# Which heads of an attention layer are turned by TensorE and which by DMA

## The reference, cut to what matters

```python
q = (x @ Wq + bq).reshape(1, B * N, H, hd)              # 1024 queries, 16 heads of 16
kv = (cond @ Wkv + bkv).reshape(1, -1, 2, H, hd)        # 1024 keys and values
q = _fq_sym(q * scale, axis=-1); k = _fq_sym(k, axis=-1); v = _fq_sym(v, axis=2)
attn = jax.nn.softmax(jnp.einsum('bhqd,bhkd->bhqk', q, k), axis=-1)
attn = _fq_unsigned(attn, axis=-1)                      # rounded to 255 levels of the row's maximum
out = jnp.einsum('bhqk,bhkd->bhqd', attn, v)
out = out.transpose(0, 2, 1, 3).reshape(B, N, C) @ Wp + bp
```

## Time and profile before

| | before |
|---|---|
| median of 3 runs | 450.31 us (449.9 to 451.88) |
| profiled execution, its own time | 452.0 us |
| its span | 450.2 us |
| PE / DVE / ACT / POOL busy | 307.4 / 365.1 / 324.3 / 124.9 us |
| mean granted TensorE clock | 0.86 of full |
| steps 0 to 127 (first to last exponential's start) | 190.98 to 378.80 us |

### The profile page before, as it was taken

One profiled execution on the slowest core, in us unless ns is written; L12 is line 12 of the kernel. 1 busy time (PEld: TensorE's weight loads), 2 busy tenths in 40 slices (PEclk: granted clock), 3 DMA queues, 4 the chain that ended last, 5 costly groups with the idle time before them and its releaser, 6 DMA issues.

```text
span 450.2 us, 7440 instructions
## 1 busy us (share of the span) xinstructions
PE 307.4 (68%) x2594; PEld 192.4 (43%) x2594; DVE 365.1 (81%) x597; ACT 324.3 (72%) x513; POOL 124.9 (28%) x260
## 2 busy tenths in 40 slices
PE   4999986774365877657577676877776777526445
PEld 2666554421264766433344443444443445203334
DVE  4758998299999683758699899899999997678975
ACT  3387689772234544799799999899999999467751
POOL 3703544000200111101212231223222312278760
PEclk9989999596596996978889999799899989755856
DMA  8600022000020001126999998889899959000001
GB/s 284 284 1 1 2 93 95 0 1 0 1 93 0 2 0 25 23 48 134 246 135 178 168 155 130 147 151 158 138 163 142 179 112 157 1 1 1 23 23 48
DMA packets 115637, 39.91 MB, mean 89 GB/s; under 512 B 110480, under 2 KB 114192, under 8 KB 114832
## 3 DMA queue, kind: packets, MB, share of 16 engines
q1 hardware_dynamic: 115168, 38.85, 43.9%
q0 software_dynamic: 144, 0.52, 0.3%
q10 hardware_dynamic: 288, 0.07, 0.1%
HBM read 11.11 MB, written 1.05 MB: 27 GB/s over the span
## 4 chain that ended last, share of the span: by engine, by line
DVE 28%; ACT 23%; PE 18%; issue 17%; POOL 9%; DMA 3%; POOLq 1%; SPq 0%; DVEq 0%; ACTq 0%
ACT rb L796 15%; DVE nm L1229 4%; POOL ra L524 4%; PE ps L1745 3%; DVE xn L895 2%; PE ps L1721 2%; POOL small L529 2%; ACT ra L850 2%; PE ps L1757 2%; DMA tern<-rb 2%; DVE rb L1154 2%; DVE rb L1141 2%; DVE gs L1132 2%; DVE rb L1152 2%; DVE st L886 1%
## 5 line engine op out<-in xcount | busy, mean ns | idle before, releaser
L1229 DVE TENSOR_REDUCE nm<-ps 128x1 f32<-128x1024 f32 x128 | 153.4, 1218 | 19.8 <-PE ps L1745 19.0
L796 ACT ACTIVATE rb<-ps,eb,sq 128x1024 int16<-128x1024 f32 x128 | 153.8, 1215 | 9.1 <-POOL eb L502 8.4
L1745 PE MATMUL ps<-ra,rb 128*128 128x512 bf16 x256 | 84.7, 418 | 41.0 <-ACT rb L796 40.4
L502 POOL TENSOR_SCALAR eb<-nm,sq 128x1 f32<-128x1 f32 x128 | 34.5, 270 | 148.5 <-DVE nm L1229 147.8
L1745 PEld LDWEIGHTS ps<-ra,rb 128*128 128x128 bf16 x256 | 16.2, 101 | 59.6 <-ACT rb L796 57.1
L1770 PEld LDWEIGHTS ps<-ra,tern 128*128 128x128 f16 x624 | 25.9, 98 | 17.5 <-issue 4.0
L1770 PE MATMUL ps<-ra,tern 128*128 128x16 f16 x624 | 26.3, 171 | 2.1 <-DMA tern<-rb 2.0
L796 ACT ACTIVATION_READ_ACCUMULATOR rb<-ps,eb,sq 128x1 f32 x128 | 27.0, 211 | 0.0
L1624 PE MATMUL ps<-xqT,tern 128*128 128x512 bf16 x64 | 19.8, 453 | 9.8 <-DVE rb L1141 8.5
L1644 PE MATMUL ps<-idb,gs 128*128 128x128 bf16 x64 | 7.7, 295 | 26.5 <-DVE gs L1324 26.5
L1757 PEld LDWEIGHTS ps<-idh,rb 128*128 128x128 f16 x256 | 17.9, 105 | 16.9 <-issue 10.6
(11 more groups left out here) (202 smaller groups left out, 727.1 us busy)
## 6 DMA issues: line engine op xcount, KB each, us to landing
stage<-w SPq DMA_DIRECT2D x2, 1024.0 KB, 4.7
rb<-ra SPq DMA_DIRECT2D x16, 128.0 KB, 2.9
rb<-wide_rows SPq DMA_DIRECT2D x1, 1536.0 KB, 7.1
xs<-x SPq DMA_DIRECT2D x4, 256.0 KB, 4.5
cx<-ctx_in SPq DMA_DIRECT2D x4, 256.0 KB, 4.7
stage<-w_gate SPq DMA_DIRECT2D x1, 1024.0 KB, 7.4
stage<-w_up SPq DMA_DIRECT2D x1, 1024.0 KB, 10.2
stage<-w_down SPq DMA_DIRECT2D x1, 1024.0 KB, 4.6
```

What stands on the lines that cost most here:

```text
L502: nc.gpsimd.tensor_scalar(eb[:, u % 3:u % 3 + 1], nm[:, u % 3:u % 3 + 1], sq[:, t, h:h + 1], LN255, ALU.mult, ALU.add).then_inc(s_bias, 1)
L796: A(esc[u % E_RING], bank(2 * (u % 3), 2), ACT.Exp, bias=eb[:, u % 3:u % 3 + 1], scale=sq[:, t, h:h + 1], accum_out=es[:, t % 2, h:h + 1]) ...
L1229: V.tensor_reduce(nm[:, u % 3:u % 3 + 1], bank(2 * (u % 3), 2), AX.X, ALU.max, negate=True).then_inc(s_max, 1)
L1745: ins = M(bank(2 * (u % 3) + hf), qz[t % 2][:, h // 2, h % 2, :], kT[:, h // 2, 512 * hf:512 * hf + 512], start=True, stop=True)
```

## The change

One constant changes, and with it who turns which head in each tile:

```diff
-ON_TENSOR = (1, 4, 12, 15)
+ON_TENSOR = (1, 6, 12)
```

## The result

The changed kernel takes 467.86 us (median of 4 runs, 462.82 to 470.24), beside 451.1 us for the kernel before on the same chip (449.9 to 452.16): 1.033 times as long, 95% interval 1.028 to 1.039. Run once more later it took 467.01 beside 452.15, 1.032 (1.027 to 1.036). The forecast was 461.0 us. 467.86 lies 0.9 us above the range of 455 to 467; the ratio on the forecast's own base, 1.033 x 450.31, is 465.3. The profile shown here is of the longest execution of the changed kernel, 470.24 us (span 468.4, clock 0.80); a second one, of 466.61 us (clock 0.82), was taken with the later run, and where the two differ both are given.

The account below looks back on a forecast made before the run. It took VectorE's maxima and ScalarE's exponentials to bound the attention loop. Tile 0 -0.45, tile 1 +0.75, even tiles +3.45, odd +5.85 and clock +1.1 made +10.7 on 450.31: 461.0 us, range 455 to 467 (own 457 to 464.5).

Parts of the forecast that it names:

- The new wait: Step 9, tiles 1 to 7: `o_transposes` waits for head 6's move on ScalarE, 1.95 us a boundary (bounds 0.47, 2.6).
- S: Start of head 8's exponential on ScalarE, from which the times at a tile's boundary are counted.
- Which wait ends last: Same boundary: head 10's exponential, behind TensorE's late scores, at S + 4.6; head 9's, about S + 2.65, is not last.
- The saved moves: Moves of heads 15 and 4 leave ScalarE: 0.8 us less per even tile, 0 in tiles 3, 5, 7.
- Tile 0: No boundary there; the move behind head 6 goes, saving 0.45 us that everything behind inherits.
- The clock: The new wait's idle stretch in each tile lowers TensorE's clock: 1.1 us in sum, bounds 0 and 10.5.
- rival C: The stall drops the clock for the heads behind it in most of seven tiles: +17.1, 467.4 us; chance 0.12.
- DMA: SP's queue keeps up, if narrowly, with 13 transposes a tile: 0, at worst 1.8 us per even tile.
- Rival B: DMA becomes the bound at 13 transposes: 1.8 us per even tile, +4.6, 454.9 us; chance 0.08.
- The end: Tile 7's head 15, now turned by DMA, lands near 383.8, before VectorE's scaling at 384.32: 0, at most 0.7 us.
- The sum: All tiles and the clock together: +10.7 us on the median 450.31, so 461.0 us.

Follow-up runs that it names:

- the filling: Changed kernel with 12 more matmuls of 256 columns, into an unread part of bank 6, ahead of each `o_transposes`: 464.94 us; again 462.95 us, 1.022 of before.

## Why the prediction was right, and where its sizes were off

*The new wait.* Right in place, releaser and count: seven waits before L1778 for L783, and none with heads 1, 4 and 12. With head 5 there are six, which cost little since they end one exponential and one move sooner. Its arithmetic for one boundary was S + 1.87 for `o_transposes` and S + 4.6 for head 10. Measured at full clock (tile 6): 4.43, so 1.79 us instead of 1.95. At the lower clock, in the six others, `o_transposes` came at S + 1.93 as well, but its two transposes, the scores (1.06 us for 0.60) and their maxima brought head 10 to S + 5.10: 2.46 us, near the bound of 2.6. I had priced all seven at full clock. This is the largest miss, 6 x 0.66 = 4.0 us (4 x 0.66 = 2.6 in the second profile). The idling itself I put at 1.5 us each, and it was 1.2; the price never hung on it.

*Which wait ends last.* Predicted, TensorE's, with head 9 "not last". Shown by `o_out` one step later: head 9 came 1.24 us sooner, head 10 not at all.

*The saved moves.* 0.8 us taken for an even tile; 0.55, 0.20 and 0.39 measured, in the second profile 0.40, 0.21 and 0.55. With head 15 alone gone heads 0 to 8 take 10.48 us (10.90 before) where the clock holds, and with head 4's move gone too at best 10.36. So the first move is worth 0.42 and the second 0.12. That behind it the turn through three pairs of banks sets the pace, as the prediction feared, fits this, but no run isolates it. In the odd tiles heads 0 to 8 stayed at 12.79 to the hundredth, as VectorE's fullness there said. Tile 1 saved 1.5 where 1.2 was forecast.

*Tile 0.* Forecast -0.45; measured +0.34, and -0.44 in the second profile. Head 6's move also stands behind head 8 there, which I had not counted: heads 8 to 10 took 2.86 us where it was 2.44. Heads 10 to 15 took 0.42 less and made up for it, so that the forecast came out by luck. In the first profile TensorE was slow at its step 9 besides, and heads 8 to 10 took 3.53.

*The clock.* I put 1.1 us on it, behind head 9, and named a fall in most tiles as rival C (467.4). What came lies between, and the larger part of C's clock came with it. The clock falls ahead of the wait: in six of seven tiles, in both profiles, the scores of step 9 already took about 1.04 us. Tile 1 is the exception, at 0.61; in the first profile the clock fell during its wait. Tile 2 of after, `o_transposes` still to come:

```profile
257.74 0.61 PE L1745 MATMUL ps<-ra,rb 128*128 128x512 bf16 x2 [0.88 <-ACT rb L796]
258.93 0.81 PE L1745 MATMUL ps<-ra,rb 128*128 128x512 bf16 x2 [0.58 <-ACT rb L796]
260.11 1.04 PE L1745 MATMUL ps<-ra,rb 128*128 128x512 bf16 x2 [0.38 <-ACT rb L796]
...
263.39 0.66 PE L1778 MATMUL ps<-idf,rb 128*128 128x128 f32 x2 [0.97 <-ACT stage L783]
```

What differs behind the wait is whether the clock is back. The scores of step 10 took 1.06 us in six boundaries of the first profile and four of the second, the ones that took 5.09 or 5.10 us, and 0.59 in the others. With the filling in the wait's place they took 0.59 to 0.62 in all seven, in both profiles, though five of the seven had come to it with scores of 1.03 us or more. So it is TensorE's idling there that keeps the clock down.

From head 10 on all tiles together lost only 0.1 us, 0.3 in the second profile, but that is luck of the comparison: tiles 1, 2 and 5 lost 2.2 us, and the profile of before had a fall of its own in tile 3, which gave 2.1 back. With the filling the same stretches took 52.9 us where the changed kernel's took 55.5 and 55.7. So the lower clock cost the changed kernel some 6 us in the first profile, 4.0 in the boundaries and 2.2 behind them, where I had put 1.1.

Steps 7 and 8 now hold nothing but scores: the `attend`s of the new tile are not due yet, and head 4's transposes, which stood at step 7, are gone. That the fall comes from this is likely and not shown: in the kernel with the filling these steps are the same, and in tiles 4 and 6 the clock held at them in both profiles. With head 5 the clock fell in the same place (tile 2) and 8 to 10 took 2.98 there, where the other tiles mostly had 2.75: little, without the wait behind it.

*DMA.* Costed at nothing for 13, right: tiles 2 and 4 in 20.9 us with 13, and at 14 a ratio of 1.003 whose interval holds 1. Rival B's sign, `attend` waiting for landed transposes, was there three times in the loop (4.9 us), as before (three, 4.4). The Trainium skill's page "DMA: Bandwidth & Descriptors", "Latency and other measured facts", gives 261 GB/s for DMA transposes with a non-contiguous middle dimension. No run here shows that rate: the busiest tile moved 178 GB/s.

*The end.* Costed at nothing; VectorE waited 0.7 us for the last `attend`, at the bound of 0.7 given.

*The sum.* In the loop +14.4 measured against +10.7: boundary 16.55 for 13.65, savings ahead of head 8 2.7 for 3.6, tile 0 +0.3 for -0.45, clock behind the boundary 0.1 for 1.1 (net of the fall that before had there). The second profile has +12.6: 15.2, 2.5, -0.4 and +0.3. The runs differ by 16.8 and, the second time, 14.9 us; what goes beyond the loop's 14.4 and 12.6 is within what the time ahead of it drifts. So the direction and the wait were foreseen and the clock's share was not: on the forecast's own base the 465.3 lies above the forecast's own range, 457 to 464.5, and nearer to C's 467.4 than to 461.0.

## What to carry to other kernels

When a piece of work moves to another slot, look at every wait that counts it: here a bank shared by two uses turned "head 6 instead of head 4" into a wait of TensorE for ScalarE, and ScalarE's next copy for TensorE, and the count in the wait moved silently with the constant. How long an engine idles doesn't price a wait; by when the next engine must have its result does: one step earlier 1.0 us of idling cost 0.15, here 0.8 to 1.8 us cost 1.8 to 2.5. Price such a step at both clocks if the scores ahead of it already run at the lower one. And take two profiles of each kernel before putting a microsecond down to a place: falls of the clock that move from tile to tile can hide one another.

## What the runs showed of the hardware that I had not expected

TensorE's granted clock fell from its upper level to its lower, half of it, while no single wait of TensorE was over 0.9 us (steps 7 to 9 above: waits of 0.88, 0.58 and 0.38 us, then scores in 1.04 us for 0.60); with 12 filling matmuls behind such scores, the next ones took 0.59 again. Behind a wait of 0.8 to 1.8 us the scores took 1.06 us in ten of the fourteen boundaries of the changed kernel's two profiles, behind the filling in none of fourteen. Two executions of one kernel put such a fall into different tiles (tile 3 in one, tile 5 in the other), at 2.2 us each, and the first exponential's start drifted between 190.98 and 195.6 us with nothing changed ahead of it.
